# A pipelined graph transformer kernel: the closing part of the later graphs is begun half a slot earlier, and its products are spread to one a step

## The chip, the cores and the metric

The program runs on one core of a Trainium2 chip. The metric is device time in microseconds (us) from start to end of one execution; lower is better. The core has TensorE (PE), VectorE (DVE), ScalarE (ACT), GpSimd (POOL) and SyncE (SP, which only issues transfers here). Each runs its own list of instructions in order; they wait for one another on semaphores.

## The reference

Eight graphs of N = 1024 nodes with C = 128 features each. A first layer takes the maximum over each node's first 25 neighbours; a second layer is masked attention with 8 heads, followed by the closing part: output projection, normalization, feed-forward network, normalization, sum with the input.

```python
h = relu(layernorm(x))
idx = top_k(where(adj != 0, -arange(N), -inf), 25)          # the first neighbours in order
agg = max over idx of h[idx]                                # the gather
x = x + relu(concat([h, agg]) @ W + b)
h = relu(layernorm(x))
allowed = (adj > 0) | (adj.T > 0) | eye
q, k, v = split(h @ Wqkv.T + bqkv)
ctx = softmax(where(allowed, q k.T / sqrt(16), -inf)) @ v   # 8 heads of 16
y = layernorm(h + ctx @ Wo.T + bo, ln1)                     # closing part from here
ff = relu(y @ W1.T + b1) @ W2.T + b2                        # 128 -> 512 -> 128
x = x + layernorm(y + ff, ln2)
```

## The kernel before

**Slots and steps.** The attention of graph g fills slot s = g, cut into 32 steps (`STEPS`); a step is one tile of 128 keys for four heads and one half (512) of the queries. Steps 0 to 15 are the near half of the queries, 16 to 31 the far half; each half has two units of 8 steps, one for each set of four heads. Four other graphs are worked on in the same slot: p = s - 1 is closed, f = s + 1 has its pooled rows put through the first layer and its queries, keys and values made, r = s + 2 has its neighbour lists ranked, l = s + 3 has them made.

**What one step is.** TensorE runs `scores(g, n)` (4 products `sc<-q_near,k_g` or `sc<-q_far,k_g`, L1674, and 16 small ones that add the mask, `sc<-barred,negident`, L1678), then `contexts` of the step before (4 products `cb<-probs,va`, L1694), then whatever else the tables put into this step. ScalarE takes two exponentials a step (`probs<-sc`, L1473), each over half of `sc`. `sc` has one set of four banks, so `scores` of the next step wait for both exponentials: `pe.wait_ge(s_probs, 2 * i)`.

**What else goes into a step** stands in tables that TensorE and ScalarE both walk:

- `FAR_AT`, `NEAR_AT`: `count_edges` and `bar` for one key tile of the far half of g or the near half of f. One such count is a 128x512 product and four or five of 128x128 (L1604 to L1609), and its result goes through ScalarE into `barred` (L1465).
- `OUTPROJ_AT`, `NT_AT`, `HID_AT`, `FFN_AT`, `SUM_AT`: the closing part of p, for each half h of the nodes: `project` (L1724), `turn_norm` (4 transposes), `hidden` (4 products with `w1T`, L1737, each read by ScalarE into `hid`, which is `wide_tiles`, L1497), `forward` (4 products with `w2T`, L1745) and `turn_sum` (4 transposes, L1753). Two `hidden` or two `forward` products share a step.
- `PROJ_AT` and step 30: queries and keys, then `value_rows` for both halves (L1779) and a small product for a flag (L1882), which waits for VectorE's `products`.
- steps 18 to 22: transposes of `hl`, of `ag` (the pooled rows), and `linear(f)`; step 25: transposes of `h2`.
- `MASK_AT`, `H_AT`: ScalarE's copies of the mask and rows of the first normalization.

All these products write one of three banks of `m`, and each waits until the bank's last content has been read (`refill`).

**VectorE's order** is written out in `middle(s)` and the loop that calls it. The part that matters here, in slot s: ... `pool_tile(f, 6)`, `context(g, 0)`, `first_norm(l)`, list tiles and merges of l, `add_input(p, 0)` (L1060), `finish(p, 0)`, `add_input(p, 1)`, `merge_pair(2)`, `finish(p, 1)`, `context(g, 1)`, `list_tile(l, 4)`, `low_levels(r)` (L974, the maximum over 13 gathered rows of the fullest tile of r), `linear(f)` (L1092 to L1099, which makes `h2`, the input of TensorE's step 25), `pool_tile(r, 0)`, `pool_tile(r, 1)`, `context(g, 2)`, `bias_ahead(f)`, and `largest(f, 0..3)` (L1112) with list tiles 5 and 6 and a merge between them, then `products(f)` (L1118). `residual(p, (0, 1))` (L1048 to L1054: sum, moments, inverse root, normalization) stands between `pool_tile(f, 4)` and `pool_tile(f, 5)`. Slots 2 to 4 have list tiles (l is a graph up to slot 4); slots 5 to 7 have none.

**GpSimd** issues the gathers: for graph f one indirect transfer for each neighbour level of each node tile (L693), held back by `paced(f, t, k)`, a wait on the count of steps, and by the buffers that VectorE has read; then the sorted rows and lists are sent (L673, L666). `beta2` (L722) is its one arithmetic instruction a graph.

Of the kernel before, what the change touches and what calls it, by code (L numbers as in the profile page):

```python
# [13 lines left out]
B, N, C = 8, 1024, 128  # L14
# [51 lines left out]
H_AT = {17: (0, 2), 19: (2, 4), 21: (4, 5), 22: (5, 8)}  # L66
H_AT_1 = {22: (0, 4), 23: (4, 8)}

OUTPROJ_AT, EARLY_OUTPROJ_AT = [{4}, {5}], {21}
NT_AT, EARLY_NT_AT = [{8}, {8}], {25}  # L70
HID_AT = [{9: [(0, 0), (1, 1)], 10: [(2, 0), (3, 1)]}, {13: [(0, 1), (1, 2)], 14: [(2, 1), (3, 2)]}]
EARLY_HID_AT = {26: [(0, 1), (1, 2)], 27: [(2, 1), (3, 2)]}
FFN_AT = [{11: 0, 12: 1}, {15: 0, 16: 1}]
EARLY_FFN_AT = {28: 0, 29: 1}
SUM_AT, EARLY_SUM_AT = [{14}, {17}], {31}
# [4 lines left out]
MASK_AT = {4: [(2, 2)], 7: [(2, 3)], 11: [(2, 4)], 12: [(2, 5)], 15: [(2, 6)], 16: [(2, 7)], 18: [(3, 0)], 21: [(3, 1)]}  # L80
MASK_AT_1 = {1: [(2, 0)], 2: [(2, 1)], 4: [(2, 2)], 6: [(2, 3)], 7: [(2, 4)], 11: [(2, 5)], 12: [(2, 6)], 15: [(2, 7)], 18: [(3, 0)], 21: [(3, 1)]}
# [106 lines left out]
def program(nc, x, adj, L0_W, L0_b, Wqkv, bqkv, Wo, bo, ln1_g, ln1_b, W1, b1, W2, b2, ln2_g, ln2_b, out):  # L188
# [6 lines left out]
    with ctx:  # L195
# [232 lines left out]
        def closing(s, n, late, early):  # L428

            pairs = []  # L430
            for h in range(2):
                if live(s - 1) and not (s == B and h == 0) and n in late[h]:
                    pairs.append((s - 1, h, late[h]))
            if s == B - 1 and n in early:
                pairs.append((s, 0, early))
            return pairs
# [15 lines left out]
        with nc.Block() as block:  # L452
# [308 lines left out]
            def _(dve):  # L761
# [547 lines left out]
                def middle(s):  # L1309
# [11 lines left out]
                    if live(f):  # L1321
                        pool_tile(f, 4)
                    if live(p):
                        residual(p, (1,) if s == B else (0, 1))
# [4 lines left out]
                    if live(l):  # L1329
                        list_tile(l, 0)  # L1330
                    if live(f):
                        pool_tile(f, 6)
                    if live(g):
                        context(g, 0)
                    if live(l):
                        first_norm(l)
                        list_tile(l, 1)
                        merge_pair(0)
                    if live(p) and s < B:
                        add_input(p, 0)  # L1340
# [4 lines left out]
                    if live(p) and s < B:  # L1345
                        finish(p, 0)
# [10 lines left out]
                    if live(g):  # L1357
                        context(g, 1)
# [4 lines left out]
                for s in range(1, B + 1):  # L1363
# [47 lines left out]
            def _(act):  # L1411
# [43 lines left out]
                def norm_out(p, h):  # L1455
                    act.wait_ge(s_nT_ready, 2 * p + h + 1)
                    nc.scalar.activation(turned[:, h * HALF:(h + 1) * HALF], m[:, h, :], ACT.Identity, bias=ln1_col[:, 1:2], scale=ln1_col[:, 0:1]).then_inc(s_nT_sb, 1)  # L1457

                def halves_out(dst, g, ready, done, func=ACT.Copy):
                    for h in range(2):  # L1460
                        half_out(dst[:, h * HALF:(h + 1) * HALF], h, ready, 2 * g + h + 1, done, func)
# [450 lines left out]
```

## Time and profile before

| | |
|---|---|
| time, three runs | 1251.53 us median (1248.22 to 1252.4) |
| the profiled execution | 1253.36 us, of which 1251.6 us are the span from the first to the last instruction |
| granted clock of TensorE, mean over the span | 0.952 |
| busy over the span | PE 1022.8 us (82%), DVE 838.7 (67%), ACT 797.7 (64%), POOL 737.4 (59%) |
| chain that ended last | PE 59%, ACT 14%, DVE 11%, POOL 6%, issue 6% |
| largest lines of that chain | L1674 20%, probs L1473 13%, L1694 11%, L1678 7% |
| step 0 of slot 2, 3, 4, 5, 6, 7 | at 469.1, 593.3, 717.5, 841.8, 966.0, 1090.2 us |
| after the last step | from 1212.7 to 1251.6 us |

Read it so: before 469 us are setup and the slots 0 and 1, then come five slots of the same length, then slot 7 and the tail in which the last graph is closed. A mean over the span says little, since the slots and the tail have different limits.

### The profile page before, as it was taken

The page shows a single profiled execution, that of the slowest core. Times are in us where ns is not written, and L with a number is a line of the kernel's source. Part 1 is how long each engine was busy: PE and PEld are TensorE (multiplying, and loading weights), DVE is VectorE, ACT ScalarE, POOL GpSimd, SP SyncE. Part 2 cuts the span into 40 slices and gives each one's busy share as a digit, 9 for nine tenths or more (in the row PEclk, how much of TensorE's full clock was granted, in tenths as well). Part 3 has the DMA queues.
Part 4 walks back from the last instruction along what each step waited for, and adds up shares of the span by engine and source line. Part 5 has one row for each costly group of instructions (what it writes and reads, how often), then busy time and mean ns, then how long its engine had stood idle before and what let it go on. Part 6 is the DMA issues. An engine that isn't in the chain of part 4 may idle for free.

```text
span 1251.6 us, 28391 instructions
## 1 busy us (share of the span) xinstructions
PE 1022.8 (82%) x10526; PEld 381.5 (30%) x10526; DVE 838.7 (67%) x3110; ACT 797.7 (64%) x1014; POOL 737.4 (59%) x741
## 2 busy tenths in 40 slices
PE   0136687588995879999999999999999999999774
PEld 0022331133321323243333333433343334333222
DVE  8866887758878576888788878887365525232424
ACT  1221257567863667788778877887768766875541
POOL 4776677557777777777777777777777620000000
PEclk9996789899998889999999999999999999999996
DMA  6533335516342524352436243522242210000000
GB/s 190 166 70 106 95 102 159 147 36 137 97 119 64 154 78 131 100 137 76 130 100 137 77 132 103 136 76 77 57 86 66 68 44 26 17 4 10 10 2 16
DMA packets 95154, 110.73 MB, mean 88 GB/s; under 512 B 17080, under 2 KB 75968, under 8 KB 94976
## 3 DMA queue, kind: packets, MB, share of 16 engines
q1 hardware_dynamic: 68352, 62.67, 16.5%
q0 software_dynamic: 22816, 44.61, 15.4%
q8 instruction: 98, 1.61, 0.5%
q10 hardware_dynamic: 3808, 1.19, 0.4%
q14 instruction: 80, 0.66, 0.2%
HBM read 91.10 MB, written 12.85 MB: 83 GB/s over the span
## 4 chain that ended last, share of the span: by engine, by line
PE 59%; ACT 14%; DVE 11%; POOL 6%; issue 6%; DMA 2%; DVEq 0%; SPq 0%; POOLq 0%
PE sc L1674 20%; ACT probs L1473 13%; PE cb L1694 11%; PE sc L1678 7%; PE m L1737 4%; PE m L1745 4%; POOL nb_low L715 3%; POOL nb_low L693 2%; PE m L1581 2%; PE m L1604 2%; PE sc L1716 2%; DVE cand L828 1%; PE m L1724 1%; PE m L1767 1%; PE m L1768 1%
## 5 line engine op out<-in xcount | busy, mean ns | idle before, releaser
L1473 ACT ACTIVATE probs<-sc 128x1024 f32<-128x1024 f32 x512 | 496.5, 1022 | 252.4 <-PE sc L1678 249.4
L693 POOL DMA_INDIRECT nb_low<-h_rows,lsorted x474 | 468.7, 989 | 173.0 <-issue 129.4
L1694 PE MATMUL cb<-probs,va 128*17 128x512 f32 x2048 | 271.6, 602 | 3.8 <-ACT probs L1473 3.4
L1674 PE MATMUL sc<-q_near,k_g 32*128 32x512 f32 x1024 | 147.4, 645 | 31.9 <-ACT probs L1473 28.8
L1674 PE MATMUL sc<-q_far,k_g 32*128 32x512 f32 x1024 | 150.5, 658 | 21.4 <-ACT probs L1473 21.0
L1014 DVE TENSOR_REDUCE agg<-nb_low 128x128 f32<-128x1024 f32 (+10 forms) x58 | 96.4, 1662 | 56.5 <-DMA nb_low<-h_rows,lsorted 30.5
L1678 PE MATMUL sc<-barred,negident 32*32 32x512 bf16 x4096 | 112.1, 388 | 0.0
L828 DVE MAX8 cand<-keys 128x8 f16<-128x128 f16 x512 | 105.3, 278 | 2.2
L715 POOL DMA_INDIRECT nb_low<-h_rows,first_lists x80 | 79.9, 999 | 41.4 <-issue 22.8
L1465 ACT ACTIVATE barred<-m 128x512 bf16<-128x512 f32 x128 | 73.4, 610 | 41.7 <-PE m L1609 41.7
L1678 PEld LDWEIGHTS sc<-barred,negident 32*32 32x32 bf16 x4096 | 35.2, 88 | 198.5 <-issue 198.5
L1484 ACT ACTIVATE m<-keys 128x1024 fp8e5<-128x1024 f16 x64 | 67.1, 1058 | 39.5 <-DVE keys L824 39.5
L824 DVE SCALAR_TENSOR_TENSOR keys<-adj_t,prio 128x1024 f16<-128x1024 int32 x64 | 77.9, 1217 | 10.3 <-DVEq L1021 6.1
L673 POOL DMA_INDIRECT pooled_rows<-agg,lsorted x56 | 62.7, 1120 | 24.3 <-issue 13.7
L1674 PEld LDWEIGHTS sc<-q_near,k_g 32*128 32x128 f32 x1024 | 40.6, 185 | 84.4 <-ACT probs L1473 58.0
L1737 PE MATMUL m<-turned,w1T 128*128 128x512 f32 x128 | 65.1, 632 | 1.0 <-ACT turned L1457 1.0
L666 POOL DMA_INDIRECT neighbour_lists<-lst,rank_i x48 | 48.7, 1014 | 28.4 <-DVE rank_i L908 15.0
L1060 DVE SCALAR_TENSOR_TENSOR turned<-m,b2c,turned 128x512 f32<-128x512 f32 x16 | 11.9, 746 | 77.8 <-PE m L1745 77.2
L1745 PE MATMUL m<-wide_tiles,w2T 128*128 128x512 f32 x128 | 63.1, 617 | 0.0
L1674 PEld LDWEIGHTS sc<-q_far,k_g 32*128 32x128 f32 x1024 | 41.0, 187 | 71.9 <-ACT probs L1473 51.4
L693 POOL DMA_INDIRECT nb_high<-h_rows,lsorted x46 | 47.4, 1030 | 14.0 <-issue 12.5
L1694 PEld LDWEIGHTS cb<-probs,va 128*17 128x17 f32 x2048 | 34.1, 95 | 62.6 <-issue 58.7
(181 smaller groups left out, 1426.2 us busy)
## 6 DMA issues: line engine op xcount, KB each, us to landing
adj_t<-in_adj_dram SPq DMA_DIRECT2D x64, 512.0 KB
nb_low<-h_rows,lsorted POOLq DMA_INDIRECT x474, 2.8
xh<-in_x_dram SPq DMA_DIRECT2D x8, 512.0 KB
h_rows<-xh SPq DMA_DIRECT2D x8, 512.0 KB
hl<-h_rows SPq DMA_DIRECT2D x8, 512.0 KB
x<-in_x_dram SPq DMA_DIRECT2D x16, 256.0 KB
out_dram<-h2T SPq DMA_DIRECT2D x16, 256.0 KB, 2.5
ag<-pooled_rows SPq DMA_DIRECT2D x7, 512.0 KB
```

The lines of the kernel that those rows point to most:

```text
L693: pool.indirect_dma_start(out=dst, out_offset=None, in_=h_rows[0:(f + 1) * (N + 1), :], in_offset=bass.IndirectOffsetOnAxis(ap=lsorted[:, ...
L715: pool.indirect_dma_start(out=first_slots(t)[:, k, :], out_offset=None, in_=h_rows[0:(f + 1) * (N + 1), :], in_offset=bass.IndirectOffsetO ...
L824: nc.vector.scalar_tensor_tensor(out=keys[:, t, :], in0=adj_t[:, t % 2, :], scalar=0.0, in1=prio[:, :], op0=ALU.not_equal, op1=ALU.mult).t ...
L828: ch.step(nc.vector.max(cand[:, t, 8 * c:8 * c + 8], keys[:, t, c * CW:(c + 1) * CW]))
L1014: ch.link(nc.vector.tensor_reduce(a, first.rearrange("p k c -> p c k"), AX.X, ALU.max))
L1465: nc.scalar.activation(barred[:, kt, half * HALF:(half + 1) * HALF], m[:, bank, :], ACT.Relu, bias=1.0, scale=-1.0).then_inc(done, 1)
L1473: nc.scalar.activation(probs[:, i % 2, 2 * pair:2 * pair + 2, :], sc[:, 2 * pair:2 * pair + 2, :], ACT.Exp, scale=SCALE).then_inc(s_probs, 1)
L1674: nc.tensor.matmul(sc[:, a, :], k[part, :], q[part, :], start=True, stop=False)
L1678: last = nc.tensor.matmul(sc[c * SPAN:(c + 1) * SPAN, a, :], negident[b, b], barred[b, kt, qh * HALF:(qh + 1) * HALF], start=False, stop=True)
L1694: last = nc.tensor.matmul(cb[a * SPAN:a * SPAN + VW, :], va[:, u % 2, a, kt, :], probs[:, i % 2, a, :], start=(kt == 0), stop=(kt == T - 1))
L1737: nc.tensor.matmul(m[:, bank, :], w1T[:, k * P:(k + 1) * P], turned[:, half * HALF:(half + 1) * HALF], start=True, stop=True).then_inc(s_h ...
L1745: last = nc.tensor.matmul(m[:, half, :], w2T[:, k, :], hid[:, k, :], start=(k == 0), stop=(k == FC - 1))
```

## The change

The tables are written for a closing part that may begin in its own slot: their step numbers count from the graph's own slot (36 is step 4 of the next). Graphs 0 and 1 keep the old places; so does graph 7. For graphs 2 to 6 (`SPREAD` = 2 and up):

- half 0: projection at step 19 and `turn_norm` at step 24 of the graph's own slot; `hidden` at 0 to 3 and `forward` at 5 to 8 of the next slot, one product a step; `turn_sum` at 11. Half 1: projection 4, `turn_norm` 8, `hidden` 9 to 12, `forward` 13 to 16, `turn_sum` 18.
- the far counts move from steps 0 to 6 to steps 1 to 14, one a step, the near counts to 16, 18, 23, 24, 26 and 31; masks and rows of the first normalization move in step with them; both transposes of `hl` go to step 17; `value_rows` is split over steps 29 and 30.
- VectorE: `residual(g, (0,))` comes right after `middle(s)`; `residual(p, ...)` keeps only half 1; `add_input(p, 0)`, `finish(p, 0)` and `context(g, 1)` come earlier; `list_tile(l, 4)` comes after `linear(f)`.

No operation is added or left out, except that `residual` runs its fixed part (the inverse root) once for each half.

```diff
-NEAR_AT = {17: [(0, 2)], 23: [(1, 2), (2, 0)], 24: [(3, 2), (4, 0)], 25: [(5, 2)], 31: [(6, 1), (7, 2)]}
+NEAR_AT = {16: [(0, 2)], 18: [(1, 2)], 23: [(2, 2), (3, 0)], 24: [(4, 0)], 26: [(5, 2)], 31: [(6, 1), (7, 2)]}
+FAR_AT_SPREAD = {1: [(0, 2)], 2: [(1, 2)], 4: [(2, 0)], 6: [(3, 2)], 10: [(4, 2)], 12: [(5, 2)], 13: [(6, 2)], 14: [(7, 2)]}
-HID_AT = [{9: [(0, 0), (1, 1)], 10: [(2, 0), (3, 1)]}, {13: [(0, 1), (1, 2)], 14: [(2, 1), (3, 2)]}]
+SPREAD = 2
+SPREAD_OUTPROJ_AT = [{19: 0}, {36: 1}]
+SPREAD_NT_AT = [{24: 2}, {40: 1}]
+SPREAD_HID_AT = [{32: [(0, 0)], 33: [(1, 1)], 34: [(2, 0)], 35: [(3, 1)]}, {41: [(0, 1)], 42: [(1, 1)], 43: [(2, 1)], 44: [(3, 1)]}]
+SPREAD_FFN_AT = [{37: (0,), 38: (1,), 39: (2,), 40: (3,)}, {45: (0,), 46: (1,), 47: (2,), 48: (3,)}]
+SPREAD_SUM_AT = [{43: 0}, {50: 1}]
...
+def values_at(f):
+
+    return (29, 30) if f > SPREAD else (30, 30)
...
-        def closing(s, n, late, early):
+        def closing(s, n, late, spread, early):
 
             pairs = []
...
+            for e in (s - 1, s):
+                for h in range(2):
+                    at = early if e == B - 1 and h == 0 else spread[h] if SPREAD <= e < B - 1 else late[h]
+                    if live(e) and STEPS * (s - e) + n in at:
+                        pairs.append((e, h, at[STEPS * (s - e) + n]))
             return pairs
...
                     if live(p):
-                        residual(p, (1,) if s == B else (0, 1))
+                        residual(p, (1,) if p >= SPREAD else (0, 1))
...
                     if live(l):
                         list_tile(l, 0)
+                    if spread:
+                        add_input(p, 0)
...
                         first_norm(l)
+                    if spread:
+                        finish(p, 0)
...
                     if live(p):
                         add_input(p, 1)
+                    if live(g):
+                        context(g, 1)
                     if live(l):
                         merge_pair(2)
                     if live(p):
                         finish(p, 1)
-                    if live(g):
-                        context(g, 1)
...
-                    if s == B - 1:
+                    if live(g) and s >= SPREAD:
                         residual(g, (0,))
-                    if live(l):
+                    if live(l) and s < SPREAD:
                         list_tile(l, 4)
                     if live(r) and s > 1:
                         low_levels(r)
                     if live(f):
                         linear(f)
+                    if live(l) and s >= SPREAD:
+                        list_tile(l, 4)
```

TensorE, slot 4, of the kernel before: the end of step 8 and step 9 (each step opens with `sc<-q_near,k_g`; what the tables add stands behind `cb<-probs,va`):

```order
L1581 MATMUL m<-identf,y 128x128 x8
L1674 MATMUL sc<-q_near,k_g 128x512 x4
L1678 MATMUL sc<-barred,negident 32x512 x16
L1694 MATMUL cb<-probs,va 17x512 x4
L1737 MATMUL m<-turned,w1T 128x512 x2
```

The same stretch of the changed kernel, the end of step 8, step 9, and step 10 up to its count, after which one L1783 follows (L1720, L1724 and L1740 are the step's own products there, L1627 to L1655 transposes and a count, L1783 `hidden`, L1791 `forward`):

```order
L1627 MATMUL m<-identf,y 128x128 x4
L1791 MATMUL m<-wide_tiles,w2T 128x512
L1720 MATMUL sc<-q_near,k_g 128x512 x4
L1724 MATMUL sc<-barred,negident 32x512 x16
L1740 MATMUL cb<-probs,va 17x512 x4
L1783 MATMUL m<-turned,w1T 128x512
L1720 MATMUL sc<-q_near,k_g 128x512 x4
L1724 MATMUL sc<-barred,negident 32x512 x16
L1740 MATMUL cb<-probs,va 17x512 x4
L1650 MATMUL m<-m,ident 128x512
L1653 MATMUL m<-ident 128x128
L1655 MATMUL m<-ident,m 128x128 x4
```

Where a step held two `hidden` products and nothing else, it now holds one, with or without a count ahead of it.

VectorE, slot 4, what stands between `finish(p, 1)` (whose last row is the first here) and `linear(f)` (L1092) before:

```order
L1080 TENSOR_TENSOR h2T<-h2T,x 128x512
L1030 STREAM_TRANSPOSE ctx_turned<-ctx_raw 128x512
L1032 RECIPROCAL rden<-ctx_turned 128x16
L1037 TENSOR_TENSOR y<-ctx_turned,rden 128x16x16
L1041 STREAM_TRANSPOSE turned<-y 128x512
L824 SCALAR_TENSOR_TENSOR keys<-adj_t,prio 128x1024
L828 MAX cand<-keys 128x8 x8
L974 TENSOR_REDUCE agg<-nb_low 128x128
L1092 SCALAR_TENSOR_TENSOR x<-m,x 128x512 x2
```

The same place in the changed kernel; the first piece ends `finish(p, 1)` and begins `residual(g, (0,))`, the second ends it, and the rows of the inverse root stand between them:

```order
L1119 TENSOR_TENSOR h2T<-h2T,x 128x512
L1087 TENSOR_TENSOR y<-h,m 128x512
L805 BN_STATS st<-y 128x6 x4
L808 BN_AGGR mv<-st 128x2 x4
L814 TENSOR_SCALAR nw<-mv 128x4
```

```order
L827 TENSOR_TENSOR nw<-mv,nw 128x4
L1093 TENSOR_SCALAR y<-y,nw 128x128 x4
L1013 TENSOR_REDUCE agg<-nb_low 128x128
L1131 SCALAR_TENSOR_TENSOR x<-m,x 128x512 x2
```

The context of the second unit and one list tile have left this place, and half a `residual` has entered it.

## Rows read from the trace of the kernel before

**Rows 1.** Busy us and instructions by window, slots 4 and 7 (PE, PEld, DVE, ACT, POOL).

```profile
717.56:841.80 124.24, 120.57 (x1298) 44.38 (x1294) 102.85 (x378) 99.02 (x127) 95.22 (x94) 1.00 0.41 112
...
1090.20:1212.70 122.50, 110.62 (x1140) 34.45 (x1135) 35.52 (x146) 78.00 (x91) 0.00 (x0) 1.00 0.03 9
```

**Rows 2.** Timeline, slot 5, step 9 (start, duration, engine; idle time in brackets).

```profile
875.35 1.98 PE L1737 MATMUL m<-turned,w1T 128*128 128x512 f32 x4
...
877.26 1.14 PE L1674 MATMUL sc<-q_near,k_g 32*128 32x512 f32 x8
877.37 0.69 ACT L1497 ACTIVATE wide_tiles<-m,b1c 128x512 f32<-128x512 f32 x1 [0.17 <-PE m L1737]
...
878.70 1.05 PE L1694 MATMUL cb<-probs,va 128*17 128x512 f32 x8
...
879.68 0.70 PE L1737 MATMUL m<-turned,w1T 128*128 128x512 f32 x1
```

**Rows 3.** Timeline, slot 5, steps 29 and 30.

```profile
954.36 1.94 ACT L1473 ACTIVATE probs<-sc 128x1024 f32<-128x1024 f32 x2 [0.18 <-PE sc L1678]
...
955.23 1.12 PE L1788 MATMUL m<-h2T,wqk 128*128 128x512 f32 x2
...
957.90 1.94 ACT L1473 ACTIVATE probs<-sc 128x1024 f32<-128x1024 f32 x2
...
958.77 2.05 PE L1779 MATMUL m<-wv,h2T 128*128 128x128 f32 x16
...
960.88 1.14 PE L1674 MATMUL sc<-q_far,k_g 32*128 32x512 f32 x8
```

**Rows 4.** Timeline of TensorE, slot 5, step 2: two counts.

```profile
849.70 0.39 PE L1604 MATMUL m<-m,ident 128*128 128x512 fp8e5 x1
...
850.15 0.38 PE L1604 MATMUL m<-m,ident 128*128 128x512 fp8e5 x1
```

**Rows 5.** The same view, step 4: the projection.

```profile
857.29 1.11 PE L1724 MATMUL m<-woT,turned 128*128 128x128 f32 x8
```

**Rows 6.** Timeline of VectorE, slot 4: `finish(p, 0)`, first and last.

```profile
775.24 0.89 DVE L766 BATCH_NORM_STATS2 st<-m 128x6 f32<-128x128 f32 x4 [1.90 <-PE m L1753]
...
781.51 0.69 DVE L1080 TENSOR_TENSOR h2T<-h2T,x 128x512 f32<-128x512 f32 x1
```

**Rows 7.** The same view: `residual`, from its second sum on.

```profile
738.18 0.69 DVE L1048 TENSOR_TENSOR y<-h,m 128x512 f32<-128x512 f32 x1 [0.36 <-PE m L1724]
...
740.58 0.64 DVE L769 BATCH_NORM_AGGREGATE mv<-st 128x2 f32<-128x6 f32 x8
...
744.03 2.23 DVE L1054 TENSOR_SCALAR y<-y,nw 128x128 f32<-128x128 f32 x8
```

**Rows 8.** The same view, from `low_levels` to the flag.

```profile
802.57 3.07 DVE L974 TENSOR_REDUCE agg<-nb_low 128x128 f32<-128x1664 f32 x1 [2.75 <-DMA nb_high<-h_rows,lsorted]
...
807.13 0.69 DVE L1092 SCALAR_TENSOR_TENSOR x<-m,x 128x512 f32<-128x512 f32 x1 [0.89 <-PE m L1768]
...
813.06 2.24 DVE L1099 TENSOR_SCALAR h<-x,nw 128x128 f32<-128x128 f32 x8
...
824.60 1.22 DVE L824 SCALAR_TENSOR_TENSOR keys<-adj_t,prio 128x1024 f16<-128x1024 int32 x1
825.86 1.64 DVE L828 MAX8 cand<-keys 128x8 f16<-128x128 f16 x8
...
834.85 0.16 DVE L1118 TENSOR_TENSOR prod<-pmax 128x1 f32<-128x1 f32 x1
836.76 0.15 DVE L1122 TENSOR_REDUCE nflag<-m 1x1 f32<-1x8 f32 x1 [1.75 <-PE m L1882]
```

**Rows 9.** Timeline of GpSimd, slot 4, step 16: two gathers.

```profile
783.32 0.94 POOL L693 DMA_INDIRECT nb_low<-h_rows,lsorted  x1 [0.30 <-issue]
784.57 0.94 POOL L693 DMA_INDIRECT nb_low<-h_rows,lsorted  x1 [0.30 <-issue]
```

**Rows 10.** Waits, 469 to 966 us: total, times, longest.

```profile
POOL neighbour_lists L666 <- DVE rank_i L908: 4.1, 3, 2.4
```

More of the change, by code:

```diff
@@ L1344, in middle @@
                         pool_tile(f, 7)
-                    if live(p) and s < B:
+                    if p < SPREAD:
                         finish(p, 0)
@@ L1738, in hidden, with forward @@
                     freed[bank] = (s_hid_sb, 2 * FC * p + c + 1)
-                def forward(p, half, part):
-                    if part == 0:
-                        refill(half)
-                    for k in range(2 * part, 2 * part + 2):
+                def forward(p, half, chunks):
+                    for k in chunks:
+                        if k == 0:
+                            refill(half)
                         pe.wait_ge(s_hid_sb, 2 * FC * p + half * FC + k + 1)
                         last = nc.tensor.matmul(m[:, half, :], w2T[:, k, :], hid[:, k, :], start=(k == 0), stop=(k == FC - 1))
-                    if part:
+                    if k == FC - 1:
                         last.then_inc(s_ffn_ready, 1)
@@ L1770, in linear, with value_rows @@
                     freed[h] = (s_lin_used, 2 * f + h + 1)
-                def value_rows(f):
-                    for h in range(2):
-                        bank = VALUE_BANK[h]
-                        refill(bank)
-                        pe.wait_ge(s_h2T_sb, 2 * f + h + 1)
-                        for t in range(TH):
-                            cols = slice((h * TH + t) * P, (h * TH + t + 1) * P)
-                            last = nc.tensor.matmul(m[:, bank, t * C:(t + 1) * C], h2T[:, cols], wv[:, :], start=True, stop=True)
-                        last.then_inc(s_v_ready, 1)
-                        freed[bank] = (s_v_sb, 2 * f + h + 1)
+                def value_rows(f, h):
+                    bank = VALUE_BANK[h]
+                    refill(bank)
+                    pe.wait_ge(s_h2T_sb, 2 * f + h + 1)
+                    for t in range(TH):
+                        cols = slice((h * TH + t) * P, (h * TH + t + 1) * P)
+                        last = nc.tensor.matmul(m[:, bank, t * C:(t + 1) * C], h2T[:, cols], wv[:, :], start=True, stop=True)
+                    last.then_inc(s_v_ready, 1)
+                    freed[bank] = (s_v_sb, 2 * f + h + 1)
                 def projection(f, j, bank):
@@ L1877, in _ @@
                                 projection(f, j, bank)
+                            for h in range(2):
+                                if n == values_at(f)[h]:
+                                    value_rows(f, h)
                             if n == 30:
-                                value_rows(f)
                                 pe.wait_ge(s_prod_ready, f + 1)
@@ L1883, in _ @@
                                 freed[0] = (s_nflag, f + 1)
-                        for e, h, _ in closing(s, n, SUM_AT, EARLY_SUM_AT):
+                        for e, h, _ in closing(s, n, SUM_AT, SPREAD_SUM_AT, EARLY_SUM_AT):
                             turn_sum(e, h)
```

100 lines of the change are left out of this document (56 added, 44 removed).

## The prediction

> **What bounds the kernel now.** I read the windows by slot first, since the mean over the span mixes slots with a tail. In slot 4 TensorE is busy 120.6 of 124.2 us, in slot 7 110.6 of 122.5 [rows 1]. Next the timeline of single steps, because a busy TensorE may still be waiting for a step's exponentials. Two lengths of step show. Step 29 has one product beside its scores and contexts: the exponentials start at 954.36 and at 957.90, 3.54 apart [rows 3]. There the loop binds: exponentials (1.94), then the next scores, which cannot start earlier. Step 9 has two products: scores begin at 877.26, contexts at 878.70, the added work at 879.68, so scores and contexts take 2.42, and two added products take 875.35 to 877.26 = 1.91 [rows 2]. So a step lasts the longer of 3.54 and 2.42 + x, with x the added TensorE work: 1.12 us is free in every step, and what goes beyond costs its whole length. Doubled steps last 4.33. That rule gives 32 x 3.54 = 113.3 for a slot; the slot has 124.2, an excess of 10.9 that sits in some 14 steps.
>
> Then the two engines behind. VectorE stands before `low_levels` 2.75 us for a gather, before the second half of `linear` 0.89, before the flag 1.75 [rows 8]: those are its margins in slot 4. GpSimd issues a gather every 1.25 us (783.32, 784.57) though each lasts 0.94 [rows 9]; slot 4 has 94 of its instructions with 95.2 us busy [rows 1], and 94 gaps of 0.30 make that 123.4 of 124.2. It is nearly full by spacing.
>
> **The change, part by part.** Prices: a product 0.96 (1.91 / 2), a count 0.45 (849.70 to 850.15) to 0.52 with its diagonal piece [rows 4], a projection at most 1.11 [rows 5], four transposes taken at one count, `value_rows` with the flag 958.77 to 960.88 = 2.11 [rows 3], so half of it about 1.0.
>
> TensorE, slots 3 to 5. Gone: eight doubled steps at 4.33 - 3.54 = 0.79, and the `turn_sum` on one of them at 0.45: 6.8. One of the two steps with projection and count, 0.45 each: 0.9 before. Step 30 at 2.42 + 2.11 - 3.54 = 1.0. With the two `linear` steps, which stay, that is the 10.9 found. These 8.7 are replaced by: product and count in one step (1, 2, 6, 10, 12, 13, 14, 16), 2.42 + 1.45 - 3.54 = 0.33 each: 2.6; step 4 0.45; steps 7, 8 and 11, a product with rank counts, transposes or `turn_sum`: 1.0; step 26, query product and count: 0.3; step 29, query product and half of `value_rows`: 2.42 + 1.96 - 3.54 = 0.85; together 5.2. The eight steps with one product only fit. Step 24 gains a third eviction on ScalarE and step 25 loses a count; taken as even. **Saved: 3.5 a slot.** Slot 6 has no ranks: 3.9. Slot 7 has neither near counts nor step 26 and 29 work: 7.8 before, 3.4 after, saved 4.4. Slot 2 still runs the doubled closing of graph 1, with a near count now on step 16 (+0.5), turned `hl` beside a `turn_sum` on 17 (+0.3) and a count on 26 (+0.3), less 0.15 at 29 and 30: +0.9. If TensorE alone decided: 0.9 - 3 x 3.5 - 3.9 - 4.4 = -17.9.
>
> VectorE. `finish` lasts 775.24 to 782.20 = 7.0 [rows 6]. Half a `residual`: sum 0.7, half of the moments (738.87 to 741.22) 1.2, inverse root (to 744.03) 2.8, half the normalization 1.1: 5.8, against 8.6 for both together [rows 7]; so 3.0 more work a slot, and 5.8 now stand in front of step 25. A list tile (2.9 [rows 8]) leaves that place. Slot 3: `turn_sum(p, 1)` ends in step 18, at 18 x 3.54 + 4.1 of excess so far + 0.9 + about 1.1 = 70; `finish(p, 1)` to 77, `residual(g, (0,))` with its waits to 83, `low_levels` 3.1 to 86, `linear` 8.8 (815.30 - 805.64 - 0.89) to 95.0 [rows 8]. TensorE wants `h2` at 25 x 3.54 + 6.3 + 0.9 = 95.7: just met. `turn_norm` in step 24 comes at 24 x 3.54 + 6.1 + 0.9 = 92, 9 after `residual` has ended. Then the list tile, now behind: 97.9, and from `h2` to `products` 815.30 to 835.01 = 19.7, less 1 us of gather waits no longer waited for: 116.6 to 117. The flag was read at 836.76, 119.2 into slot 4 and 5.0 before its end; with 3.5 saved it would be 115.7, and it cannot be before 117 + 0.5. So **1.8 of the 3.5 come back** as a wait of TensorE in step 30: slot 3 saves 1.7. The cover of `residual` is VectorE's idle time; what is queued behind TensorE's wait is the next slot's scores, for which ScalarE waits.
>
> Slot 4: the gather that `low_levels` waits for landed at 85.0 of the slot. GpSimd does not speed up with the steps; its waits for `rank_i` (4.1 us over three [rows 10]) give back a few tenths. So it lands at about 85.3 of a slot that begins earlier; VectorE is there at 83 and waits 2.2, `h2` comes at 97.3 (TensorE waits about 1), `products` at 119.1, the end at 119.1 + 5.5 = 124.6: saves nothing (+0.4). Slot 2, without the spread half: `finish(p, 1)` from 72.8, `residual` to 86, `products` near 120, flag about 0.4 late: +1.3. Slots 5 to 7 have no list tiles: VectorE reaches `low_levels` at 83, finds its gather there, and is idle before the flag.
>
> Sum: +1.3 - 1.7 + 0.4 - 3.5 - 3.9 - 4.4 = **-11.8**. The profiled execution took 1253.4, giving 1241.6; from the median 1251.5, which is 1.8 lower, 1239.7. I say 1241.
>
> The tail is in program order as before: no term.
>
> A rule that speaks against the full gain, and one for it. The Trainium skill (Perfetto Trace Analysis, Identifying the Most-Contended Engine) judges GpSimd by occupancy; by that it has 29 us a slot to spare and only VectorE holds the slots up. The same page (GPSIMD Engine Instruction) calls its spans unreliable and asks for start-to-start spacing; by that GpSimd is full. The row of two gathers, 1.25 apart, agrees with the second; by the first the sum would be that of TensorE and VectorE, about 1.5 us lower.
>
> **Rivals.**
> A: TensorE alone decides (VectorE's margins are larger than I chain them): -17.9, 1235.5. For it: waits of 2.75 and 1.75 in slot 4; against: the 3.0 us of new work and its place.
> B: GpSimd binds in slots 3 to 5. These can then only shrink by its idle time, about 1 us beyond what is forced each, and slot 5's 3.5 are lost too: 1.3 - 1.0 - 0.5 + 0 - 3.9 - 4.4 = -8.5, 1245. For it: 123.4 of 124.2. Against: its results (except for `low_levels`) are used well after they land.
> C, slower: VectorE's chain before step 25 does not hold. Were the 5.8 of `residual` wholly added in slots 2, 3 and 4 in front of `h2`, the list tile's place being no help because VectorE was waiting there for the gather anyway, then these slots last 124.2 + 5.8 minus the 0.9 it had waited: +14.7, less 11.8 from slots 5 to 7: +2.9; if slot 5 stalls too, +8, 1256 to 1262. It decides from about 4 us of delay a slot.
> D, also slower: the one bank. Half 1's four products now all go through bank 1, each waiting for the eviction (0.69, and 0.17 behind the product [rows 2]) of the one before. By the chain above the eviction ends 2.7 after a step's exponentials begin and the next product comes at 4.4, so it is hidden by 1.7. Were it exposed, 4 x 0.86 a slot over five slots is +17, 1258. The Trainium skill (Perfetto Trace Analysis, Optimizing Tensor Performance) asks that independent products rotate through banks; the change goes the other way for these four.
> E: it does not spread the load: single-product steps take 3.8, not 3.54, because ScalarE's evictions and masks stand behind the exponentials; some 9 such steps in five slots cost 0.26 each, +12, so no change. Step 29, with two evictions of 1.45, still has 3.54 [rows 3]; that speaks against it.
>
> **How the numbers follow.** My forecast (-9.5 to -14.5) 0.47; A 0.14; B 0.20; E and other mixtures near no change 0.09; C 0.07; D 0.03. The range takes in A and B: 1234 to 1248, leaving out 0.19. What a measurement of this kernel tells from no change is 0.3%, 3.8 us: faster takes the forecast, A, B and a little of the mixtures, 0.83; same 0.08; slower 0.09.
>
> **What would show it.** Steps 9, 11, 15 at or near 3.54 to 3.8 instead of 4.33; steps 1, 2, 6, 10, 12 to 14 and 16 near 3.87; step 29 near 4.4 and step 30 at 3.5 plus a wait for VectorE's `prod` in slots 2 to 4 and none later; slots 5 to 7 at about 120.7, 120.3, 118.1; slots 2 to 4 at about 125.5, 122.5, 124.6. `low_levels` with no wait in slots 2, 3 and 5 and about 2 in slot 4. I am wrong if TensorE waits at step 25 for `h2` over 2 us, at step 20 for bank 1 (held by `finish(p, 1)`, margin under 1 us), or at 23 for bank 0 (held by `linear`'s first half, margin under 1.5), all three behind the same VectorE chain.

## The result and the profile after

The changed kernel takes 1254.6 us (median of 16 runs, 1251.37 to 1258.04), the kernel before 1249.95 (16 runs, 1247.96 to 1253.59). The ratio is 1.0034, with a 95% interval of 1.0023 to 1.0044: some 4 us slower, where 1241, some 10 us faster, was forecast.

The windows view of the changed kernel, slots 2 to 7, against [rows 1] and the steady 124.2 of before (columns: window and length, then PE, PEld, DVE, ACT, POOL busy with instructions, PEclk, DMA share, GB/s):

```profile
464.40:591.60 127.20, 121.81 (x1310) 46.11 (x1311) 105.75 (x393) 99.46 (x127) 95.33 (x94) 1.00 0.40 110
591.60:721.50 129.90, 124.05 (x1298) 44.84 (x1302) 106.45 (x393) 99.34 (x127) 94.54 (x94) 0.97 0.41 106
721.50:850.30 128.80, 122.69 (x1298) 43.77 (x1297) 107.13 (x400) 99.31 (x126) 94.04 (x92) 0.99 0.40 108
850.30:971.50 121.20, 120.68 (x1298) 43.91 (x1302) 70.66 (x232) 93.99 (x117) 92.34 (x95) 1.00 0.30 71
971.50:1092.10 120.60, 120.08 (x1288) 43.16 (x1284) 54.32 (x186) 88.27 (x111) 36.15 (x35) 1.00 0.16 43
1092.10:1210.60 118.50, 109.81 (x1128) 32.12 (x1122) 32.65 (x133) 77.34 (x90) 0.00 (x0) 1.00 0.03 9
```

Two halves are to be seen. Slots 5 to 7, which have no list tiles, are 121.2, 120.6 and 118.5 long: forecast 120.7, 120.3 and 118.1. Slots 2 to 4, forecast at 125.5, 122.5 and 124.6, take 127.2, 129.9 and 128.8. They lose 13.3 us against the forecast and 13.3 against the kernel before; slots 5 to 7 gain 10.6. The profiled execution took 1252.2 us against 1253.4, but its slot 2 also begins 4.7 us earlier, behind slots 0 and 1 which run the same program (in the 13 profiled executions, all alike up to there, slot 2 began between 463.5 and 469.1 us); the medians average over that chance.

The load is spread as the tables say. ScalarE's timeline of the changed kernel, steps 9 and 10 and then step 29 of slot 5, answers to [rows 2, 3]: exponentials at 884.42 and 887.96, so step 9 with one product has 3.54; step 10 with product and count 3.93; step 29, 4.36.

```profile
884.42 1.94 ACT L1520 ACTIVATE probs<-sc 128x1024 f32<-128x1024 f32 x2 [0.77 <-PE sc L1724]
886.45 0.69 ACT L1544 ACTIVATE wide_tiles<-m,b1c 128x512 f32<-128x512 f32 x1
887.96 1.94 ACT L1520 ACTIVATE probs<-sc 128x1024 f32<-128x1024 f32 x2 [0.82 <-PE sc L1724]
...
891.89 1.94 ACT L1520 ACTIVATE probs<-sc 128x1024 f32<-128x1024 f32 x2 [0.76 <-PE sc L1724]
...
959.93 1.94 ACT L1520 ACTIVATE probs<-sc 128x1024 f32<-128x1024 f32 x2 [0.18 <-PE sc L1724]
961.96 1.45 ACT L1550 ACTIVATE q_far<-m,bqk,packed_rows 128x512 f32<-128x512 f32 x2
964.29 1.94 ACT L1520 ACTIVATE probs<-sc 128x1024 f32<-128x1024 f32 x2 [0.88 <-PE sc L1724]
```

So the time went in slots 2 to 4. The waits of the changed kernel over these three (engine, line, what it waited for: total, times, longest) say on whom:

```profile
POOL pooled_rows L712 <- DVEq L1062: 16.5, 4, 7.9
...
DVE agg L1013 <- DMA nb_high<-h_rows,lsorted: 7.2, 2, 4.1
...
PEld m L1824 <- DVE amax L1151: 5.8, 3, 3.1
...
PEld m L1929 <- DVE prod L1157: 4.3, 2, 2.5
```

The first is the new one. GpSimd's send of the pooled rows of f (L712; L673 before) waits for VectorE's `pool_tile(f, 7)`. In slots 3 and 4 it stood 16.1 us in three waits; in the same slots of the kernel before, 1.1 in three, at most 0.4. GpSimd's timeline of slot 3 shows it:

```profile
643.39 2.07 POOL L712 DMA_INDIRECT pooled_rows<-agg,lsorted  x1 [0.30 <-issue]
653.35 1.96 POOL L712 DMA_INDIRECT pooled_rows<-agg,lsorted  x1 [7.88 <-DVEq L1062]
655.62 1.01 POOL L732 DMA_INDIRECT nb_low<-h_rows,lsorted  x1 [0.30 <-issue]
...
668.18 0.94 POOL L732 DMA_INDIRECT nb_low<-h_rows,lsorted  x1 [0.30 <-issue]
669.43 0.94 POOL L732 DMA_INDIRECT nb_low<-h_rows,lsorted  x1 [0.30 <-issue]
```

VectorE's timeline of the same slot: `finish(p, 0)` ends with the row at 642.75, list tiles 1 and 2 follow, then the pooling of tile 7, a wait for the gather in front of `low_levels` and one in front of `pool_tile(r, 1)`:

```profile
642.75 0.69 DVE L1119 TENSOR_TENSOR h2T<-h2T,x 128x512 f32<-128x512 f32 x1
643.36 1.22 DVE L863 SCALAR_TENSOR_TENSOR keys<-adj_t,prio 128x1024 f16<-128x1024 int32 x1
...
651.46 1.25 DVE L1053 TENSOR_REDUCE agg<-nb_low 128x128 f32<-128x640 f32 x1
...
678.01 3.07 DVE L1013 TENSOR_REDUCE agg<-nb_low 128x128 f32<-128x1664 f32 x1 [3.01 <-DMA nb_high<-h_rows,lsorted]
...
698.91 2.69 DVE L1053 TENSOR_REDUCE agg<-nb_low 128x128 f32<-128x1408 f32 x1 [3.69 <-DMA nb_low<-h_rows,lsorted]
```

GpSimd stood still from 645.5 to 653.35, and from there on it issues one gather after the other, 1.25 us apart, with no pause in which to catch up; every gather behind the send is late, and with it whatever waits for a gather. VectorE then waits, and TensorE waits for VectorE. TensorE's timeline, slot 3, step 29 and the next scores:

```profile
705.56 1.13 PE L1833 MATMUL m<-h2T,wqk 128*128 128x512 f32 x2 [1.66 <-DVE amax L1151]
708.96 2.08 PE L1824 MATMUL m<-wv,h2T 128*128 128x128 f32 x8 [2.27 <-DVE amax L1151]
710.97 2.09 PE L1720 MATMUL sc<-q_far,k_g 32*128 32x512 f32 x8
```

ScalarE stood 5.51 us for the next scores behind this, so step 29 alone took 10.7 us instead of 4.4. Not all of that is waiting. TensorE had stood 1.66 us and was standing again when its granted clock fell to 0.50, the lower of its two levels (1.2 GHz); it stayed there from 708.1 to 714.9 us (columns as above):

```profile
708.10:714.90 6.80, 5.94 (x40) 2.60 (x40) 6.73 (x34) 1.29 (x3) 5.28 (x6) 0.50 0.39 124
```

The scores take 2.09 us there against 1.14 at full clock [rows 2], and the eight products of `value_rows` 2.08 against 1.05 in the kernel e5 below. So of the 6.4 us that step 29 is too long, some 4 are waits and some 2 the clock. The kernel before has no such stretch in slots 2 to 7, nor has e5. The changed kernel has 10.2 us of it in slots 3 and 4, where TensorE is busy 4.7 us longer in all than in the same slots of e5.

### The profile page after: what moved, and what is told of

Its sections match the earlier page's. It is cut to its first block, busy times and chain, and to the rows that moved or that the text cites. A ratio compares the mean times of both kernels' runs of the same rounds, so it can differ in the third digit from the quotient of the medians.

```text
span 1250.0 us, 28464 instructions
## 1 busy us (share of the span) xinstructions
PE 1021.9 (82%) x10526; PEld 376.5 (30%) x10526; DVE 852.2 (68%) x3185; ACT 797.5 (64%) x1014; POOL 736.6 (59%) x741
## 4 chain that ended last, share of the span: by engine, by line
PE 58%; DVE 15%; ACT 8%; POOL 7%; issue 7%; DMA 5%; DVEq 1%; SPq 0%; POOLq 0%; ACTq 0%
PE sc L1720 18%; PE cb L1740 13%; ACT probs L1520 7%; PE sc L1724 6%; PE m L1783 5%; PE m L1791 5%; POOL nb_low L754 3%; POOL nb_low L732 2%; DMA nb_low<-h_rows,lsorted 2%; DVE cand L867 2%; PE m L1650 2%; PE m L1627 2%; DVE agg L1053 2%; DVE keys L863 2%; PE m L1655 1%
## 5 line engine op out<-in xcount | busy, mean ns | idle before, releaser
L1740 PE MATMUL cb<-probs,va 128*17 128x512 f32 x2048 | 272.7, 604 | 3.6 <-ACT probs L1520 3.0
L1720 PE MATMUL sc<-q_far,k_g 32*128 32x512 f32 x1024 | 151.0, 660 | 17.7 <-ACT probs L1520 16.9
L1720 PE MATMUL sc<-q_near,k_g 32*128 32x512 f32 x1024 | 147.2, 645 | 18.5 <-ACT probs L1520 16.2
L1724 PE MATMUL sc<-barred,negident 32*32 32x512 bf16 x4096 | 112.6, 390 | 0.0
L1724 PEld LDWEIGHTS sc<-barred,negident 32*32 32x32 bf16 x4096 | 35.3, 88 | 199.0 <-issue 199.0
L712 POOL DMA_INDIRECT pooled_rows<-agg,lsorted x56 | 64.7, 1156 | 41.4 <-DVEq L1062 27.1
L863 DVE SCALAR_TENSOR_TENSOR keys<-adj_t,prio 128x1024 f16<-128x1024 int32 x64 | 78.0, 1219 | 12.1 <-DVEq L1060 8.8
L1783 PE MATMUL m<-turned,w1T 128*128 128x512 f32 x128 | 69.9, 644 | 1.0 <-ACT turned L1504 1.0
L1720 PEld LDWEIGHTS sc<-q_near,k_g 32*128 32x128 f32 x1024 | 40.4, 184 | 89.7 <-ACT probs L1520 78.2
L1791 PE MATMUL m<-wide_tiles,w2T 128*128 128x512 f32 x128 | 67.3, 624 | 0.0
L1720 PEld LDWEIGHTS sc<-q_far,k_g 32*128 32x128 f32 x1024 | 41.0, 187 | 61.1 <-ACT probs L1520 48.3
L1650 PE MATMUL m<-m,ident 128*128 128x512 fp8e5 x128 | 52.1, 407 | 3.4 <-DVE x L1131 2.4
```

Source lines behind the costliest of these rows:

```text
L863: nc.vector.scalar_tensor_tensor(out=keys[:, t, :], in0=adj_t[:, t % 2, :], scalar=0.0, in1=prio[:, :], op0=ALU.not_equal, op1=ALU.mult).t ...
L1650: nc.tensor.matmul(o, ident8[:, :], m1[:, f % GRAPHS, kt, half * HALF:(half + 1) * HALF], start=True, stop=False)
L1720: nc.tensor.matmul(sc[:, a, :], k[part, :], q[part, :], start=True, stop=False)
L1724: last = nc.tensor.matmul(sc[c * SPAN:(c + 1) * SPAN, a, :], negident[b, b], barred[b, kt, qh * HALF:(qh + 1) * HALF], start=False, stop=True)
L1740: last = nc.tensor.matmul(cb[a * SPAN:a * SPAN + VW, :], va[:, u % 2, a, kt, :], probs[:, i % 2, a, :], start=(kt == 0), stop=(kt == T - 1))
L1783: nc.tensor.matmul(m[:, bank, :], w1T[:, k * P:(k + 1) * P], turned[:, half * HALF:(half + 1) * HALF], start=True, stop=True).then_inc(s_h ...
```

## The experiments

Theory 1 says that the late `pool_tile(f, 7)` and GpSimd's send behind it cost the time. Theory 2 says that VectorE's added work, the residual's half in front of `h2` above all, does. The first four kernels ran on one chip, with the kernel before at 1251.12 us.

**e1_finish_back.** `finish(p, 0)` goes back behind `pool_tile(f, 7)`; all else stays as changed.

```diff
                     if live(l):
                         first_norm(l)
-                    if spread:
-                        finish(p, 0)
...
                     if live(f):
                         pool_tile(f, 7)
-                    if p < SPREAD:
+                    if p < SPREAD or spread:
                         finish(p, 0)
```

> One part undone: finish(p, 0) goes back behind pool_tile(f, 7) on VectorE; all else as in the changed kernel. Theory 1 (the send): GpSimd stands 7.9 us in slots 3 and 4 before it sends the pooled rows of tile 7, because pool_tile(f, 7) now comes about 8 us later on VectorE, and the next graph's gathers start that much later. Then the wait goes to under 1 us, slots 3 and 4 fall from 129.9 and 128.8 to 122 to 125, slot 2 stays near 127, and the kernel is 9 to 12 us under the changed one, so 5 to 8 us under the one before. Theory 2 (VectorE's extra work: 3 us a slot and half a residual in front of step 25): VectorE does the same work, so the time stays within 2 us of the changed kernel.

Measured: 1245.89 us, ratio 0.9954 (0.9937 to 0.9971). The time came as theory 1 said, the details less so: the send still stands 4.2 us in two waits (under 1 expected), and slots 3 and 4 are 125.7 and 126.1 long (122 to 125). **e2_pool7_ahead** makes the same cure from the other side: `finish` stays where the change put it, and `pool_tile(f, 7)` comes ahead of list tile 2.

```diff
                     if live(l):
                         list_tile(l, 1)
+                    if spread and live(f):
+                        pool_tile(f, 7)
+                    if live(l):
                         merge_pair(0)
...
-                    if live(f):
+                    if live(f) and not spread:
                         pool_tile(f, 7)
```

> finish(p, 0) stays early, but pool_tile(f, 7) moves up on VectorE by a merge and a list tile (5.2 us), to right behind list_tile(l, 1). Theory 1: GpSimd's wait before the send falls from 7.9 to 2 to 3 us in slots 3 and 4, which shrink by about 4 us each: 7 to 10 us under the changed kernel. Theory 2: the same work on VectorE, within 2 us of the changed kernel.

Measured: 1245.41 us, ratio 0.9954 (0.9937 to 0.9971). Both are about 10 us below the changed kernel (1.0034 - 0.9954 = 0.8%), and 5 to 6 us below the kernel before. The line of the send for the kernel with `pool_tile(f, 7)` ahead, slots 3 and 4, shows what fell, from 16.1 in three waits to 5.5 in two:

```profile
L712 POOL DMA_INDIRECT pooled_rows<-agg,lsorted x16: 973/996/2069, 601.0 to 839.7; - x16
its engine sat idle before it (us, times) until:
  DVEq L1062: 5.5, 2
```

In this kernel the residual half and the early `finish` are all still there. Slots 3 and 4 are 126.1 and 124.8 long, 7.8 us less than in the changed kernel. Theory 1 holds for most of the loss.

**e3_before_pool7_late** is the same test without the change: the kernel before, with `finish(p, 0)` and `pool_tile(f, 7)` swapped.

```diff
-                    if live(f):
-                        pool_tile(f, 7)
                     if live(p) and s < B:
                         finish(p, 0)
+                    if live(f):
+                        pool_tile(f, 7)
```

> The kernel before with one thing changed: in slots 2 to 6 pool_tile(f, 7) comes behind finish(p, 0) on VectorE, some 8.5 us later; no work added, TensorE and ScalarE untouched. Theory 1: the send waits 6 to 8 us in each of slots 2 to 5, and since GpSimd had at most 1 to 4 us idle a slot, these slots grow by 3 to 6 us each: 12 to 20 us over the kernel before. Theory 2: VectorE's work and its place before step 25 are unchanged, within 2 us of the kernel before.

Measured: 1278.35 us, ratio 1.0208 (1.0184 to 1.0231), 26 us slower by the swap of two neighbours in VectorE's order. The send's line for this kernel, slots 2 to 5, and the windows of its slots 2 and 3:

```profile
  DVEq L1023: 40.9, 4
```

```profile
468.90:599.20 130.30, 122.39 (x1299) 44.51 (x1296) 100.40 (x361) 99.20 (x127) 92.79 (x91) 0.99 0.38 105
599.20:734.70 135.50, 125.40 (x1299) 45.40 (x1295) 103.33 (x400) 99.35 (x127) 97.98 (x96) 0.96 0.39 104
```

The send stood 40.9 us in four slots; slots 2 to 5 grew by 6.1, 11.3, 5.9 and 3.2 = 26.5. So the loss is about two thirds of what GpSimd stands. Both are larger than expected. The swap also puts VectorE's wait for TensorE's `turn_sum` in front of the pooling (3.0, 5.5 and 3.0 us in slots 2 to 4), so the send waits 9.1 to 11.1 us each time and not 6 to 8. And part of the loss is the clock: over these four slots TensorE is busy 491.1 us against 482.1 before, with four stretches, 17.0 us in all, at a granted clock of 0.50.

The loss does not come from the late pooled rows themselves: steps 18 to 22, which turn them and put them through `linear`, keep their lengths. It stands mostly at steps 23 and 30, behind VectorE, which waits 8.0 to 12.1 us in front of `low_levels` for the late gathers.

**e4_list4_back.** In the changed kernel `list_tile(l, 4)` returns to its old place in front of `low_levels`; `pool_tile(f, 7)` stays late.

```diff
-                    if live(l) and s < SPREAD:
+                    if live(l):
                         list_tile(l, 4)
...
-                    if live(l) and s >= SPREAD:
-                        list_tile(l, 4)
```

> In the changed kernel list_tile(l, 4) goes back in front of low_levels and linear, so VectorE has 2.9 us more in front of step 25 in slots 2, 3 and 4. Theory 1: in slots 3 and 4 VectorE stands there 3 to 4 us for a gather anyway, so nothing changes in them; only slot 2 can grow, by up to 2.9; 0 to 3 us over the changed kernel. Theory 2: each of the three slots grows by 2.9, 7 to 9 us over the changed kernel.

Measured: 1249.6 us, ratio 0.9986 (0.9971 to 1.0): 6 us faster than the changed kernel. Both theories had the sign wrong here. Slot 2 falls from 127.2 to 125.5, its step 30 from 5.4 to 3.6; slot 3 falls from 129.9 to 127.1, while the send still stands 15.8 us. Slot 4 stays at 128.6: its loss only moves from steps 29 to 31 to steps 20, 23 and 24. The list tile was in an idle stretch: VectorE would have waited there for the gather anyway [rows 8]. Behind `linear` it stands in front of `largest` and `products`.

The second four ran with the kernel before at 1251.32. **e8_before_list4_late** does only that move, in the kernel before:

```diff
-                    if live(l):
+                    if live(l) and s < 2:
                         list_tile(l, 4)
...
                     if live(f):
                         linear(f)
+                    if live(l) and s >= 2:
+                        list_tile(l, 4)
```

> The kernel before with one part of the change alone: list_tile(l, 4) moved behind linear(f) from slot 2 on. By the prediction's reckoning (a list tile that leaves the place in front of low_levels helps) nothing is lost, since TensorE has no wait there: within 1 us. By the reading of the last run, VectorE stands about 2.9 us longer for the gather instead, and largest, products and the flag come 2.9 us later; products stood 1.4 us ahead of TensorE, so step 30 grows by 1.5 us in slots 2, 3 and 4: 3 to 5 us slower.

Measured: 1258.66 us, ratio 1.0058 (1.0041 to 1.0076), 7 us slower, where 3 to 5 were expected. Its waits over slots 2 to 4:

```profile
DVE agg L974 <- DMA nb_high<-h_rows,lsorted: 18.3, 3, 6.4
...
PEld m L1884 <- DVE prod L1118: 5.5, 3, 2.2
PE m L1884 <- DVE prod L1118: 4.9, 3, 2.0
```

In front of `low_levels` VectorE now stands 18.3 us in three slots, against 6.8 before: the move emptied the place and the wait filled it. The flag then comes late in each slot; step 30 takes 6.1, 7.8 and 5.9 instead of 4.5 (the 7.8 with 3.4 us at a granted clock of 0.50 behind the wait). That is one cost in two kernels, with the same sign.

**e5_both.** The changed kernel with the two edits of e2 and e4 together (their diffs stand above).

> The changed kernel with both of the edits that helped singly: pool_tile(f, 7) right behind list_tile(l, 1) and list_tile(l, 4) back in front of low_levels. If the late send and the late list tile are two separate costs, their gains add: 9 us and 5 us from 1254.6, so about 1241, slots 2 to 4 together about 8 to 10 us shorter than in the changed kernel (377 down to some 370), step 30 of slot 2 at 3.5. If both edits only remove the same wait (VectorE late at the flag), the result is that of the better one alone, about 1245.

Measured: 1241.14 us, ratio 0.9916 (0.9897 to 0.9935). The two single gains were 1.0034 - 0.9954 = 0.80% and 1.0034 - 0.9986 = 0.48%; together 1.18%, so they add nearly in full. The send now stands 5.5 us in three waits, `low_levels` and the flag are near time, and the windows of slots 2 to 5 are:

```profile
463.50:589.00 125.50, 121.77 (x1310) 46.16 (x1311) 105.63 (x394) 99.43 (x127) 95.29 (x94) 1.00 0.40 110
589.00:712.80 123.80, 121.04 (x1298) 43.87 (x1299) 105.98 (x393) 99.20 (x127) 93.88 (x93) 1.00 0.42 112
712.80:836.20 123.40, 121.03 (x1298) 43.84 (x1295) 105.50 (x393) 99.17 (x127) 94.21 (x93) 1.00 0.42 112
836.20:957.30 121.10, 120.57 (x1298) 43.82 (x1294) 71.91 (x238) 93.95 (x116) 92.41 (x96) 1.00 0.30 72
```

This is the spread load as it was meant, 10 us below the kernel before. What is left of theory 2 can be read in it: in slot 3 step 23 takes 4.1, step 25 4.3 and step 30 5.0, against 3.5, 3.5 and 3.6 in slot 5. By the unrounded lengths that is 0.5 + 0.8 + 1.4 us of VectorE's lateness. How much of it belongs to the residual's half and how much to the list tile beside it is not shown: no run moved the residual's half alone.

**e6_pool7_first** and **e7_list5_early** go on from there.

e6 is e5 with:

```diff
+                    if spread and live(f):
+                        pool_tile(f, 7)
                     if live(l):
                         list_tile(l, 1)
-                    if spread and live(f):
-                        pool_tile(f, 7)
-                    if live(l):
                         merge_pair(0)
```

and e7 is e6 with:

```diff
                     if live(r):
                         pool_tile(r, 0)
+                    if live(l) and s >= SPREAD:
+                        list_tile(l, 5)
+                    if live(r):
                         pool_tile(r, 1)
...
-                    if live(l):
+                    if live(l) and s < SPREAD:
                         list_tile(l, 5)
```

> As the kernel with both edits, and pool_tile(f, 7) one place further ahead, right behind finish(p, 0): VectorE reads it at about 642.8 of the earlier trace instead of 645.6, and GpSimd's send, which still stood 2.9 and 2.6 us, stands less than 0.5. If GpSimd is full to the brim in these slots, each microsecond of its wait is one of the slot: 2 to 5 us less over slots 3 and 4, about 1237. If VectorE's late part (list tiles 5 and 6 in front of the flag) is what remains, no change beyond 1 us.

> As the one before, and list_tile(l, 5) drawn ahead of pool_tile(r, 1), where VectorE stood 3.5 us for a gather in the trace of the changed kernel with pool_tile(f, 7) ahead. If VectorE is late at step 29 and 30 because it stands there and does the list tile afterwards, the 2.9 us list tile fills the wait and value_rows and the flag come up to 2.9 us earlier in each of slots 2 to 4: steps 29 and 30 from 7 and 6 to near 4.4 and 3.5, 3 to 6 us less in all. If the gathers themselves come late for want of GpSimd time, pool_tile(r, 1) is later by as much as the list tile takes beyond the gather, and the result stays within 1 us.

Measured: 1240.46 us, ratio 0.9914 (0.9895 to 0.9934), and 1241.61 us, ratio 0.9915 (0.9897 to 0.9933). Neither differs from e5. In e6 the send's waits fall from 5.5 to 2.6 us, and slots 3 and 4 only from 123.8 and 123.4 to 123.7 and 123.0: the last 3 us of that wait were worth half a microsecond. The expectation that each microsecond of it is one of the slot (2 to 5 us less) failed: a short wait of GpSimd is absorbed, the long ones were not. In e7 step 30 of slots 3 and 4 falls from 4.8 and 4.3 to 4.3 and 3.6, but step 1 of slot 5 grows from 3.9 to 5.2. So step 30 was relieved, and the time stayed.

The last three ran with the kernel before at 1251.6. **e9_list4_late_again** is e7 with `list_tile(l, 4)` behind `linear(f)` in slots 3 and 4, **e11_list6_alone** is e7 with `list_tile(l, 6)` behind `flag(f)` and `pool_tile(r, 2)`, **e10_list6_last** has both.

The move of e9 and e10, and that of e11 and e10:

```diff
-                    if live(l):
+                    if live(l) and s <= SPREAD:
                         list_tile(l, 4)
...
                         linear(f)
+                    if live(l) and s > SPREAD:
+                        list_tile(l, 4)
```

```diff
-                    if live(l):
+                    if live(l) and s < SPREAD:
                         list_tile(l, 6)
...
                         pool_tile(r, 2)
+                    if live(l) and s >= SPREAD:
+                        list_tile(l, 6)
```

> The kernel with list_tile(l, 5) drawn ahead, and list_tile(l, 4) behind linear(f) again in slots 3 and 4, the place that cost 5 us in the changed kernel. There VectorE had no wait in front of low_levels and was 0.9 us late with h2 in step 25 and 0.5 in step 23. If a list tile costs only where it leaves an idle stretch, step 25 is back at 3.5 and low_levels waits no more than 2 us, since the gather is there some 2 us after the residual's end; but products, which were just in time (0.3 us), come about 2 us later and step 30 grows by it: in sum within 1 us, 1241. If its place behind linear is bad in itself, some 3 us slower, 1244.

> The kernel with list_tile(l, 5) drawn ahead, and list_tile(l, 6) behind flag(f) and pool_tile(r, 2) in slots 2 to 4: products come 4 us earlier in the slot. If VectorE at the flag is still a bound, step 30 of slot 3 falls from 4.3 to 3.5 and the time by about 1 us. If GpSimd is the bound now (four slots of 122.3 to 123.2 us with 94 to 97 instructions at 1.25 us, idle in all for under 2 us a slot), nothing: slots 3 to 5 keep 368 us together and the time is 1241 within 1 us.

> Both of these edits. If VectorE is the bound, step 25 and step 30 are both relieved: slots 3 and 4 at 121 us, about 3 us less than with list_tile(l, 5) ahead alone, 1238. If GpSimd's spacing is the bound, the slots cannot get below about 94 x 1.25 = 118 plus its unavoidable waits of 2 to 4 us, and nothing or under 1 us comes: 1241.

Measured: 1241.62 us, ratio 0.9917 (0.9901 to 0.9934); 1241.32, 0.9922 (0.9909 to 0.9935); 1239.7, 0.9907 (0.9893 to 0.9922). All three lie within the interval of e5. In e9 step 25 is at 3.5 again and step 30 of slot 3 at 6.9 instead of 4.3: the same 2.9 us of list tile, moved from one wait to another. The residual's half is in its place in this kernel, and steps 23 and 25 do not wait. In e11 step 30 is at 3.6, but step 3 of slots 3 and 4 grows from 3.6 to 4.5 and 4.9; in e10, where it grows as well, TensorE's wait there is for VectorE's `full`, which now stands behind the list tile. Only with both moves are steps 23, 25 and 30 of slots 3 and 4 all at 3.5 to 3.6; the windows of slots 3 to 5 of e10:

```profile
591.20:713.30 122.10, 120.86 (x1300) 43.92 (x1302) 106.26 (x393) 98.85 (x126) 92.99 (x93) 1.00 0.42 113
713.30:836.20 122.90, 120.88 (x1298) 43.79 (x1297) 105.65 (x393) 98.84 (x126) 94.34 (x94) 1.00 0.41 113
836.20:958.70 122.50, 120.75 (x1298) 43.95 (x1302) 74.64 (x247) 94.07 (x117) 93.34 (x96) 1.00 0.31 72
```

TensorE has 120.8 busy in each, which is the floor that slot 5 of the changed kernel shows (121.2). GpSimd's 93, 94 and 96 instructions with 0.30 between them come to 92.99 + 27.9 = 120.9, 122.5 and 122.1: it is as full as TensorE. Step 1 of slot 5 takes 5.2 us in e7 and e10: TensorE's contexts stand 1.2 us there, although their exponentials were long done. SyncE's loads of `va`, which they read, began 0.3 us later in e7 than in e5 (837.68 and 837.38), and issuing the first two took 1.98 us instead of 1.13; that these hold the step is likely, not shown. From 121.2 to these 122.1 to 122.9, some 1 or 2 us a slot are left to a better order of VectorE (an estimate).

## Why the prediction was wrong

The forecast was -11.8 us; the medians say +4.

- **TensorE's prices held.** Steps of one product took 3.54, product and count 3.9 (forecast 3.87), step 29 4.4 (forecast 4.4). The three slots without list tiles saved 10.6 in the profile, where 11.8 were forecast: the step shown with a product and a count takes 3.93, not 3.87. Neither E nor D happened: steps 9 and 15, with one product each, are at 3.5. Step 11, named with them as a sign, takes 3.9; the prediction's own sum had it among the steps with a product and transposes.
- **The step that failed** is the part on VectorE for slots 2 to 4, "Sum: +1.3 - 1.7 + 0.4", and the sentence that shielded it, against B: GpSimd's "results (except for `low_levels`) are used well after they land". It asks who waits for GpSimd and never for whom GpSimd waits. I had priced `finish(p, 0)`'s new place by what TensorE wants of VectorE (`h2`, banks, flag) alone. The move puts 7.0 us [rows 6] in front of `pool_tile(f, 7)`; behind that one stands the send, and behind the send, in one queue, every gather of the next graph. The waits of 7.88 and 7.91 us in slots 3 and 4 are a little more than the 7.0 moved. e1 and e2 take most of them away and give 10 us back; e3 produces them in the kernel before and costs 26. No term of the sum had the granted clock either: it fell behind TensorE's long waits and made them dearer.
- **The text held the number that made it dear**: 123.4 of 124.2 us by spacing. I used it only to say that GpSimd does not get faster (B), not that a microsecond lost there never comes back. "`low_levels` with no wait in slots 2, 3 and 5 and about 2 in slot 4" was wrong by it: 3.0 in slot 3, 4.1 in slot 4. The Trainium skill (Perfetto Trace Analysis, GPSIMD Engine Instruction) asks to read GpSimd by start-to-start spacing; the experiments agree, since by its busy time of 95 us a slot an 8 us wait would have vanished in 29 us of slack.
- **`list_tile(l, 4)` had the wrong sign.** The prediction counted its leaving the place ahead of `low_levels` as a help. For slots 2 to 4 it was a loss: 6 us by e4 and 7 by e8. Its own rows [rows 8] showed VectorE idle 2.75 us there. Rival C spoke this very sentence ("the list tile's place being no help because VectorE was waiting there for the gather anyway") and then used it only for `h2`. The loss lands at the flag, step 30: slot 2, forecast at +1.3, came at +3.0, and e4 with the tile back gives +1.3 there (125.5).
- **C, the slower rival**, had the right sign by another mechanism. The residual's half in front of `h2` costs at most what e5 shows at steps 23 and 25, 1.3 us in slot 3, not 5.8; with the list tile away (e9) these steps show nothing. C's second sum does not add up either: if slot 5 loses the same 4.9 and not only its 3.5, that is 8.4 on top of +2.9, not +8 in all.
- **Its signs of being wrong**: of the three steps named, 25 came 0.9 us late in slots 3 and 4 (limit 2), 20 was on time, and 23 was late, 0.8 and 1.8 us. There TensorE waited for the bank that `linear`'s first half holds (L1650 for L1131, 2.4 us in two waits). The prediction had all three behind VectorE's chain of work; in slots 3 and 4 that chain itself stood 3.0 and 4.1 us for the gather.
- **B** stood for a GpSimd that only limits the gain. With the two orders put right (e5) the forecast's own number is met, 1241.14 against 1241, but for a kernel that is not the one predicted; in it slots 2 to 4 are at 125.5, 123.8 and 123.4, near the forecast 125.5, 122.5 and 124.6.

## What to carry to other kernels

Before moving an instruction on one engine, list every engine that waits for what now stands behind it, the queues that only issue transfers too; a nearly full in-order queue hands much of a long wait on to the end of its period (here 26.5 of 40.9 us, the clock's part included; of a last 3 us, half a microsecond). Work that stands in front of a wait is free, and taking it away moves nothing forward: look at the idle time in front of the next instruction before counting its leaving as a gain. And test a large reordering by its parts, since here two misplaced blocks of VectorE's order cost some 15 us and turned a gain of 10 us into a loss of 4. When TensorE waits long, read the granted clock behind the wait: here the wait cost more than its own length.

## What the runs showed of the hardware that was not expected

An arithmetic instruction on GpSimd stretches a tiny one on VectorE. VectorE's and GpSimd's timeline of the changed kernel, slot 4:

```profile
761.73 0.17 DVE L822 TENSOR_TENSOR nw<-nw 128x8 f32<-128x8 f32 x1
...
761.94 3.07 DVE L823 TENSOR_TENSOR nw<-nw 128x8 f32<-128x8 f32 x1
...
762.59 2.37 POOL L761 TENSOR_TENSOR x<-x,bias_rows 128x1024 f32<-128x1024 f32 x1
```

The product of 128x8 elements, 0.17 us otherwise, lasts 3.07 and ends with GpSimd's sum (765.01 and 764.96), though it began 0.65 us before it. The Trainium skill (SBUF — State Buffer, Who interferes with whom) has VectorE's two-input operations contend with a GpSimd instruction that reads the same memory, and lets the one that issues first go first; the row agrees with the first, while the second it does not show. It lies in the first normalization of l, and the change did not bring it: the kernel before has the same in slots 2 to 4 (2.92 to 2.95 us). In slot 3 of e3 GpSimd's sum (643.50 to 645.87) falls beside MAX8 and MATCH_REPLACE8 instructions of a list tile, and none of them is stretched.
